# Gathering a graph layer's features as fp32 rows instead of three bf16 parts

## What is computed

```
h = relu(rgcn(layernorm(x), basis0, comp0, root0, bias0))
h = relu(rgcn(h,            basis1, comp1, root1, bias1))
x = x + (lin_w[type of node] applied to h) + lin_b[type]
x = x + ffn(layernorm(x))      # 8 experts, the best two of each node weighted by a softmax

rgcn: W_r = sum_b comp[r, b] * basis_b                    # 8 relations, 4 bases
      msg = (x W_r)[src of edge],  r = type of edge
      agg = sum over r of the mean of msg over the edges of relation r that end in the node
      out = agg + x @ root + bias
```

## Time and profile before

| | |
|---|---|
| median of 3 runs | 4842.9 us (4841.7 to 4844.9) |
| profiled execution | 4840.0 us |
| its span, first to last instruction | 4838.2 us |
| TensorE products, busy | 3842.3 us, 79% |
| TensorE weight loads, busy | 3300.8 us, 68% |
| GpSimd, busy | 3331.7 us, 69% |
| VectorE, busy | 3017.5 us, 62% |
| ScalarE, busy | 881.8 us, 18% |
| moved | 749 MB, 155 GB/s |
| mean granted clock of TensorE | 0.78 of 2.4 GHz |

### The profile page before, as it was taken

One profiled execution on the slowest core, in us unless ns is written; L12 is line 12 of the kernel. 1 busy time (PEld: TensorE's weight loads), 2 busy tenths in 40 slices (PEclk: granted clock), 3 DMA queues, 4 the chain that ended last, 5 costly groups with the idle time before them and its releaser, 6 DMA issues.

```text
span 4838.2 us, 119647 instructions
## 1 busy us (share of the span) xinstructions
PE 3842.3 (79%) x38119; PEld 3300.8 (68%) x38120; DVE 3017.5 (62%) x6579; ACT 881.8 (18%) x2470; POOL 3331.7 (69%) x3374
## 2 busy tenths in 40 slices
PE   1366666666666666666469999999999999999999
PEld 1255555555555555555358888888888888888888
DVE  4556656666666566666456666666666666666663
ACT  1200000000000000000013333333333333333333
POOL 0477777777777777777477676767676777676770
PEclk6555555555555555555569999999999999999999
DMA  4656655555555555555465555555555555555551
GB/s 129 192 171 183 176 158 156 157 158 158 155 157 159 156 157 158 158 156 157 117 169 166 156 159 155 158 154 158 154 158 156 158 157 160 154 160 154 159 158 22
DMA packets 344661, 749.10 MB, mean 155 GB/s; under 512 B 128323, under 2 KB 167806, under 8 KB 344430
## 3 DMA queue, kind: packets, MB, share of 16 engines
q0 software_dynamic: 215040, 662.09, 48.7%
q1 hardware_dynamic: 115510, 70.49, 5.6%
q10 hardware_dynamic: 14076, 16.04, 1.0%
HBM read 719.00 MB, written 29.35 MB: 155 GB/s over the span
## 4 chain that ended last, share of the span: by engine, by line
PE 59%; issue 12%; DVE 12%; POOL 9%; DMA 8%; DVEq 0%; SPq 0%; ACT 0%; POOLq 0%; ACTq 0%
PE bank L1351 15%; PE bank L1338 14%; PE bank L1251 11%; POOL slot L558 9%; PE bank L1283 8%; DMA slot<-table,idx 6%; DVE inv L939 4%; PE bank L1247 3%; DVE scaled L945 3%; PE bank L1311 3%; PE bank L1312 2%; DVE mixed L913 2%; PE bank L1279 1%; DVE inv L938 1%; PE bank L1314 1%
## 5 line engine op out<-in xcount | busy, mean ns | idle before, releaser
L558 POOL DMA_INDIRECT slot<-table,idx x3354 | 3326.0, 992 | 1342.0 <-issue 1085.2
L1251 PE MATMUL bank<-hot,slot 128*128 (+1 forms) x21168 | 1380.1, 212 | 67.5 <-DMA slot<-table,idx 60.6
L1251 PEld LDWEIGHTS bank<-hot,slot 128*128 128x128 bf16 x21168 | 1112.1, 108 | 219.4 <-issue 75.0
L1247 PE MATMUL bank<-hot,ones_b 128*128 x1764 | 398.7, 226 | 745.4 <-DMA slot<-table,idx 340.1
L1338 PE MATMUL bank<-xnT,ffn_w 128*128 128x128 f32 x6272 | 867.1, 285 | 20.0 <-DVE scaled L945 20.0
L1247 PEld LDWEIGHTS bank<-hot,ones_b 128*128 128x128 bf16 x1764 | 181.0, 103 | 1006.4 <-issue 969.2
L1351 PE MATMUL bank<-ffn_w,act 128*128 128x256 f32 x3136 | 842.0, 395 | 0.3 <-DVE o L1024 0.3
L1338 PEld LDWEIGHTS bank<-xnT,ffn_w 128*128 128x128 f32 x6272 | 755.8, 192 | 46.4 <-DVE scaled L945 28.8
L1351 PEld LDWEIGHTS bank<-ffn_w,act 128*128 128x128 f32 x3136 | 541.1, 191 | 60.7 <-issue 16.9
L913 DVE SCALAR_TENSOR_TENSOR mixed<-scaled,small,mixed 128x256 f32<-128x256 f32 x1372 | 573.7, 480 | 12.2
L913 DVE SCALAR_TENSOR_TENSOR mixed<-scaled,comp_sb,mixed 128x256 f32<-128x256 f32 x1372 | 573.5, 480 | 10.5
(11 more groups left out here) (148 smaller groups left out, 2192.0 us busy)
## 6 DMA issues: line engine op xcount, KB each, us to landing
slot<-table,idx POOLq DMA_INDIRECT x3354, 3.1
inv<-inv_d SPq DMA_DIRECT2D x98, 256.0 KB, 3.8
table<-ffn_w SPq DMA_DIRECT2D x7, 1344.0 KB, 6.0
table<-parts ACTq DMA_DIRECT2D x49, 192.0 KB, 3.1
ffn_w<-in_L_ffn_W_dram SPq DMA_DIRECT2D x16, 512.0 KB
xcur<-in_x_dram SPq DMA_DIRECT2D x48, 128.0 KB
out_dram<-o ACTq DMA_DIRECT2D x48, 128.0 KB
ffn_w<-in_x_dram SPq DMA_DIRECT2D x6, 896.0 KB, 9.0
```

The lines of the kernel that those rows point to most:

```text
L558: gp.indirect_dma_start(out=slot[:, k, :], out_offset=None, in_=table[layer], in_offset=bass.IndirectOffsetOnAxis(ap=idx[:, h, k:k + 1], a ...
L1247: t.matmul(C[:, at], ones_b[:, :], oh, start=(k == 0), stop=(k == TILES - 1), skip_group_check=True)
L1251: last = t.matmul(S[f][:, at], slot[:, k, q * D + f * P:q * D + (f + 1) * P], oh, start=(k == 0 and q == 0), stop=(k == TILES - 1 and q == ...
```

## The change

Both tables are fp32, 256 numbers or 1024 bytes a row. A gather brings a tile of 128 x 256 fp32. The one-hot tile `hot` and the matrix of ones are fp32 too. Each tile takes two fp32 products (and one for the counts in the first layer) in place of six (and one). Nothing is split: `group_parts`, the copy L636, `rest` and both `parts` steps are gone, `store_group` stores the normalised rows as they are once they are made, and `publish` stores one fp32 copy of the turned result. `slot` is now 18 x 256 fp32 within a buffer of the old size. The normalising of group g now waits for the store of group g - 2, since it overwrites what that store reads. Index tables, gathers, their number, blocks, bases of tiles and the order of all else stay.

```diff
--- before
+++ after
@@
-PARTS = 3
@@
-        table = [dram("table0", (NPAD, PARTS * D), BF16), dram("table1", (NPAD, PARTS * D), BF16)]
+        table = [dram("table0", (NPAD, D), F32), dram("table1", (NPAD, D), F32)]
@@
-        slot = sb("slot", [P, TILES, PARTS * D], BF16)
+        EARLY = TILES * 384
+        early = sb("early", [P, EARLY], F32)
+        slot = early[:, 0:TILES * D].rearrange("p (t d) -> p t d", t=TILES)
@@
-        hot = sb("hot", [P, 2, TILES, COLS], BF16)
+        hot = sb("hot", [P, 2, TILES, COLS], F32)
@@
             def store_group(i, g):
-                sp.wait_ge(g_hi, g + 1)
-                sp.wait_ge(g_mid, g + 1)
-                sp.wait_ge(g_lo, g + 1)
+                sp.wait_ge(g_norm, g + 1)
...
-                sp.dma_start(dst_ap, gparts[i].rearrange("p t q d -> p t (q d)")).then_inc(g_out[i], 16)
+                sp.dma_start(dst_ap, xn[i]).then_inc(g_out[i], 16)
@@
                     act_.wait_ge(g_Tc, g - 1)
-                    act_.wait_ge(g_rest, g - 1)
+                    act_.wait_ge(g_out[i], 8 * (g - i))
                 for t in range(GROUP):
...
                 last.then_inc(g_norm, 1)
-                act_.wait_ge(g_norm, g + 1)
-                if not isinstance(g, int) or g >= 2:
-                    act_.wait_ge(g_out[i], 8 * (g - i))
-                sc.activation(gparts[i][:, :, 0, :], xn[i], ACT.Copy).then_inc(g_hi, 1)
-
@@
             def publish(p):
                 act_.wait_ge(hT_done, p + 1)
-                act_.wait_ge(parts_out, p * 16)
-                sc.activation(parts[:, 0, :], T2[:, 0:D], ACT.Copy).then_inc(hi_done, 1)
-                act_.wait_ge(rest_done, START + p + 1)
-                sc.activation(parts[:, 1, :], rest[:, :], ACT.Copy).then_inc(mid_done, 1)
-                act_.wait_ge(lo_done, START + p + 1)
-                act_.wait_ge(mid_done, START + p + 1)
+                act_.wait_ge(rows_out, p * 16)
+                sc.activation(turned[:, :], T2[:, 0:D], ACT.Copy).then_inc(hi_done, 1)
+                act_.wait_ge(hi_done, START + p + 1)
                 act_.dma_start(tab_p[bass.ds(p, 1), :, :].rearrange("a p d -> (a p) d"),
-                               parts[:, :, :].rearrange("p q d -> p (q d)")).then_inc(parts_out, 16)
+                               turned[:, :]).then_inc(rows_out, 16)
@@
-            def group_parts(i, g):
...
@@
-            group_parts(0, 0)
             ch0 = ch.n - 2 * GL
             with dve.Fori(1, (GROUPS - 1) // 2) as g2:
                 for i in range(2):
                     ch.begin(g2 * (2 * GL) + (ch0 + i * GL))
                     group_stats(i, g2 * 2 + i)
-                    group_parts(1 - i, g2 * 2 + i - 1)
@@
                 v.tensor_copy(featT[:, :, bass.ds(p * P, P)],
                               ROOTED[:, 0:D].rearrange("p (k n) -> p k n", k=HALVES)).then_inc(feat_saved, 1)
-                dve.wait_ge(hi_done, p + 1)
-                dve.wait_ge(mid_done, START + p)
-                dve.wait_ge(lo_done, START + p)
-                v.tensor_tensor(rest[:, :], T2[:, 0:D], parts[:, 0, :], ALU.subtract).then_inc(rest_done, 1)
-                dve.wait_ge(mid_done, START + p + 1)
-                v.tensor_tensor(parts[:, 2, :], rest[:, :], parts[:, 1, :], ALU.subtract).then_inc(lo_done, 1)
@@
                     if self.layer == 0:
-                        t.matmul(C[:, at], ones_b[:, :], oh, start=(k == 0), stop=(k == TILES - 1),
+                        t.matmul(C[:, at], ones_f[:, :], oh, start=(k == 0), stop=(k == TILES - 1),
                                  skip_group_check=True)
                     for f in range(HALVES):
-                        for q in range(PARTS):
-                            last = t.matmul(S[f][:, at],
-                                            slot[:, k, q * D + f * P:q * D + (f + 1) * P], oh,
-                                            start=(k == 0 and q == 0), stop=(k == TILES - 1 and q == PARTS - 1),
-                                            skip_group_check=True)
+                        last = t.matmul(S[f][:, at], slot[:, k, f * P:(f + 1) * P], oh, start=(k == 0),
+                                        stop=(k == TILES - 1), skip_group_check=True)
@@
             def turn(p):
                 pe.wait_ge(relu_done, START + p + 1)
-                pe.wait_ge(rest_done, START + p)
+                pe.wait_ge(hi_done, START + p)
```

55 lines of the change are left out of this document (14 added, 41 removed).

## The result

| | before | after |
|---|---|---|
| median | 4843.9 us (4 runs, 4841.7 to 4845.9) | 5556.0 us (4 runs, 5513.6 to 5594.6) |
| ratio | | 1.147 (95%: 1.139 to 1.155) |
| profiled execution | 4840.0 us, span 4838.2 | 5513.6 us, span 5511.4 |

The kernel is slower by 712 us, 170 more than forecast (5386) and 106 over the upper end of the range. The runs of after also lie 81 us apart, those of before 4. The profiled execution of after is its fastest one, so where the two traces are compared, 673 us are to be explained.

What follows compares the result with a forecast made beforehand. Gathers were taken to bound the first layer, TensorE the second: 4840 + 335 (second layer) + 226 (first layer) - 18 (start) = 5383, with the median 2.9 us above the profiled execution 5386 us; range 5125 to 5450.

Steps and rivals of the forecast that it cites:

- Second layer, +335: Second layer, bound by TensorE at full clock: dearer fp32 tiles add 7.2 us a pair, +335 us in all.
- Load-paced records: TensorE products: the weight load sets the pace, 0.1116 us a record at full clock, 0.215 at half.
- no wait in return: Second layer: TensorE is 99% busy, so no waiting time is there to absorb the added work.
- The rival by which streaming sets the pace: Both layers: a 64-column record takes 0.056 us, half of a 128-column one; 4787 to 4904 us in all, chance 0.04.
- Start, -18: Before the first gather: VectorE loses three passes a group, ScalarE one; -18 us, or only -8 if loads and stores hold back.
- GpSimd: Gathers: GpSimd's 946 ns a gather stays unchanged with 1024-byte rows in place of 1536.
- the gathers didn't get shorter: Rival for first-layer gathers: they shorten with their rows, -173 us given full clock, 4987 us in all; chance 0.03.
- First layer, +226: First layer: even blocks at half clock, odd at full; a pair takes 49.0 us, 4.7 over the gathers, +226 us.
- the joint: First layer, from a block's last tile to the next block's first: 6.9 us, transform or turn inside.
- The mixed clock: The forecast's own first-layer case, one block of a pair at each clock: 5386 us, chance 0.44.
- the lost clock: First-layer rival: odd blocks lose the full clock after 2.9 us, pairs 57.6 us, +638, 5798 us; chance 0.13.
- The free first layer: First-layer rival: close fp32 tiles bring full clock, 37.8 us a pair fits under the gathers; 5160 us, chance 0.36.

Runs made afterwards that it cites:

- the kernel that has none: Changed kernel with three more fp32 products of 128 columns behind each transform of the first layer: 5407.5 us, ratio 1.117.

## Why the prediction was wrong

- **Second layer, +335.** Right, 333 between the marks, and 332 where it was changed alone. Load-paced records, 0.19 us a single tile, no wait in return: all as worked out, and moving twice the columns left the price alone. The rival by which streaming sets the pace fell with it.
- **Start, -18.** Right: -17.0, the last normalising ends at 149.5 (forecast 147), the first gather comes at 156.4.
- **GpSimd.** Right: 0.95 us a gather whatever the bytes of a row, and the gathers didn't get shorter.
- **First layer, +226: the step that failed.** It is the sentence "I carry this over: tiles alone don't bring the full clock [...]; the transform does; and new tiles, standing close, keep it". Its first two parts held. The third held in 35 of 48 odd blocks in one trace and 32 in the other; in the rest the clock fell 2.0 to 2.8 us into the block. Narrow tiles behind the transform keep the clock only where the joint behind it has little idle time and the rise came late. The working put the joint at a fixed 6.9 us with the transform inside and never asked how much of it TensorE stands idle after the transform. That idle time was 0 to 1.1 us and went with the moment at which the clock had risen, which shifts from step to step. With 34 x 49.4 + 13 x 57.7 + 39.2 = 2469 us the stretch is met to 1 us. The lengths of both kinds of step, 49.0 and 57.6, were right to 0.4 us. Of the 129 us between these traces that the forecast lacks, 13 x 8.3 = 108 are the long steps. Another 16 are the three blocks ahead of the first transform, a term that the sum put at nothing, though no transform stands there to lift the clock; some 4 are the rest.
- **The form of the forecast.** "Which it is depends on the clock" was answered once for all 48 pairs. The mixed clock got 0.44, the lost clock 0.13, each as a whole kernel's time, and the range, built of whole cases, left out all between 5450 and 5798. A state that can change from step to step gives a share and a spread. The first trace less its 13 long steps is 5513.6 - 13 x 8.3 = 5406 us, close to the 5407.5 of the kernel that has none; from there the eight runs, 5514 to 5613 us, stand for 13 to 25 long steps.
- **Rivals.** The free first layer, held at 0.36, did not come with this kernel, but it is real at 128 columns. In the stretch from 705.5 to 756.6 us weight loads were under way for 46.6 of 51.1 us and the clock stayed at half; the same loads with 128 columns lifted it. The Trainium skill ("TensorE: Matmul & The Clock Gate", "What's actually happening") left open whether a weight load is busy time for the clock; by these rows weight loads without a pause don't lift it, and the columns streamed count. The 2.6 in the rival on streaming is a slip: the working's own prices, 0.446 and 0.257 us a tile, give 1.7.

## What to carry over

Where an engine's clock has two levels and the work comes in rounds, ask of each round what decides the level, and forecast a share and a spread, not a state; where one round sets the next one's level, expect runs of the same state. A product that is paced by its weight load streams up to 128 columns for the same time, and the columns can be worth having for the clock alone: here 128 columns in place of 64 took 230 us off the changed kernel, and three idle products at the right joint 134. In work that TensorE bounds at the full clock, count the fp32 weight loads, 0.11 us each, two a product, before trading bf16 products for them.

## What was not expected

- More work made the kernel faster twice: three products more behind each transform, -134 us and runs 3.5 us apart; twice the columns, -230 us.
- 1.4 us of VectorE's time at one joint cost 4.7 us a pair, since 34 in place of 16 of the 48 odd blocks lost the clock.
- A gather that meets a VectorE pass of 2.55 us takes 2.56 to 3.1 us in place of 0.95; neither the form of the pass nor cutting it in six helped.
- On some chips the kernel before takes 6090 us in place of 4840, with TensorE idle for no reason that the profile shows.
